# A small transformer layer with routed experts: the attention step's products, transposes and copies in another order

## The reference

```
h = gamma * norm(word[ids] + pos + type[types]) + beta       # eps 1e-12
a = norm(h)
q, k, v = a @ Wq, a @ Wk, a @ Wv         # 16 heads of 16
q, k = headnorm(q) * qw + qb, headnorm(k) * kw + kb
attn = softmax(causal(q k^T / 4))
h = h + (attn @ v) @ Wo + bo
x = norm(h)
scores = softmax(x @ gate^T); the 2 best experts of scores + bias
h = h + sum of the two: score * (silu(xs @ w1[e]) * (xs @ w3[e])) @ w2[e],  xs = x * score
```

## Time and profile before

| | |
|---|---|
| median of 3 runs | 560.64 us (559.51 to 562.48) |
| the profiled execution | 562.17 us |
| its span, first to last instruction | 560.0 us |
| mean granted TensorE clock | 0.958 |
| attention steps with scores | 29.9 to 201.8 us of the span |
| experts | from about 244 us on |

### The profile page before, as it was taken

How to read it: one execution, slowest core, us unless ns; L and a number is a source line. 1 busy time by engine, 2 the same in 40 slices (tenths; PEclk the granted TensorE clock), 3 DMA queues, 4 the chain that set the end, 5 groups by cost and what they waited for, 6 DMA issues and landing times.

```text
span 560.0 us, 12788 instructions
## 1 busy us (share of the span) xinstructions
PE 509.3 (91%) x4212; PEld 431.8 (77%) x4213; DVE 286.1 (51%) x710; ACT 258.1 (46%) x591; POOL 270.3 (48%) x503
## 2 busy tenths in 40 slices
PE   6788999999999886289999999999999999999991
PEld 2345767776777674169999999999999999999981
DVE  3686888788887656933333333333333333333330
ACT  1068899989988872043223332233322333322320
POOL 4587786777663201142444444443444444444432
PEclk9899999999999986589999999999999999999996
DMA  4017611000137673001211222112221122222221
GB/s 161 9 51 270 205 39 57 28 28 28 56 123 226 198 228 121 20 29 30 32 28 37 38 38 36 24 35 38 38 38 28 29 38 38 38 29 29 37 38 20
DMA packets 29480, 36.62 MB, mean 65 GB/s; under 512 B 7792, under 2 KB 23024, under 8 KB 29456
## 3 DMA queue, kind: packets, MB, share of 16 engines
q0 software_dynamic: 8352, 12.76, 13.3%
q1 hardware_dynamic: 20288, 22.51, 12.3%
q10 hardware_dynamic: 816, 1.06, 0.5%
HBM read 26.81 MB, written 9.50 MB: 65 GB/s over the span
## 4 chain that ended last, share of the span: by engine, by line
PE 81%; DVE 6%; POOL 3%; issue 3%; DMA 3%; ACT 3%; ACTq 0%; POOLq 0%; DVEq 0%
PE PS L1276 34%; PE PS L1287 18%; PE PS L1060 10%; PE PS L1146 7%; PE PS L1227 3%; PE PS L1107 3%; PE PS L1122 2%; PE PS L1099 2%; DMA x_pair<-word_dram,idx 1%; ACT work L566 1%; PE PS L1159 1%; DMA out_dram<-x_pair,dst_c 1%; DVE front L785 1%; DMA work<-x_rows,src_c 1%; POOL rstd L398 1%
## 5 line engine op out<-in xcount | busy, mean ns | idle before, releaser
L1276 PEld LDWEIGHTS PS<-work,arena 128*128 128x128 f32 x1716 | 197.6, 192 | 3.8 <-ACT work L670 2.0
L1276 PE MATMUL PS<-work,arena 128*128 128x128 f32 x1716 | 198.1, 276 | 1.5 <-ACT work L670 1.5
L676 ACT ACTIVATE work<-PS 128x768 f32<-128x768 f32 x39 | 31.6, 810 | 197.2 <-PE PS L1276 197.2
L1287 PE MATMUL PS<-w_sb,work 128*128 x468 | 107.6, 380 | 0.7 <-DVE x_pair L1035 0.7
L1027 DVE TENSOR_TENSOR work<-work,PS 128x640 f32<-128x640 f32 x39 | 32.0, 822 | 139.5 <-ACT work L676 139.5
L1287 PEld LDWEIGHTS PS<-w_sb,work 128*128 128x128 f32 x468 | 86.1, 191 | 11.0 <-issue 1.1
L513 POOL DMA_INDIRECT out_dram<-x_pair,dst_c x39 | 79.9, 2048 | 22.0 <-POOL dst_c L512 20.5
L566 ACT ACTIVATE work<-PS,nmax 128x128 f32<-128x128 f32 x256 | 72.5, 403 | 4.5 <-DVE nmax L795 4.5
L512 POOL COPY dst_c<-dest_i 128x1 int32 (+1 forms) x39 | 7.1, 182 | 137.2 <-DVE x_pair L1035 134.9
L666 ACT ACTIVATE arena<-w_sb 128x1408 f32 x40 | 55.1, 1377 | 17.8 <-DVE er_i L1000 12.8
L1060 PE MATMUL PS<-ident,work 128*128 128x128 f32 x336 | 56.5, 283 | 2.8 <-ACT work L566 2.6
(11 more groups left out here) (147 smaller groups left out, 610.4 us busy)
## 6 DMA issues: line engine op xcount, KB each, us to landing
w_sb<-w_dram SPq DMA_DIRECT2D x16, 640.0 KB, 6.2
w_sb<-w_dram SPq DMA_DIRECT2D x8, 704.0 KB, 4.7
x_rows<-x SPq DMA_DIRECT2D x16, 128.0 KB, 1.9
out_dram<-arena SPq DMA_DIRECT2D x16, 128.0 KB, 2.1
w_sb<-w_dram SPq DMA_DIRECT2D x16, 64.0 KB, 6.3
w_sb<-w_qkv_dram ACTq DMA_DIRECT2D x1, 768.0 KB, 7.9
work<-x_rows,src_c POOLq DMA_INDIRECT x41, 2.8
out_dram<-x_pair,dst_c POOLq DMA_INDIRECT x39, 4.2
```

The lines of the kernel that those rows point to most:

```text
L1276: last = n.matmul(up_ps[p][:, i, c, :], ws[p][:, k, at:at + P], xT_sb[p][:, k, :], start=(k == 0), stop=(k == DK - 1))
L1287: last = n.matmul(PS[:, 7, 0:D], hT_sb[p][:, i, :], w2_sb[:, bass.ds(e, 1), i, :], start=(i == 0), stop=(i == FK - 1))
```

## The change

- **Banks.** The transposes of `a_n` go to the right half of `VY_BANK`. `outputs` no longer waits for `aT_ready`, but for `var_f`, the reader of the output product in the right half of `O_BANK`, in every step; the rows' transposes and `values` wait for each other's readers in `VY_BANK` (`v_ready`, `aT_ready`).
- **TensorE's order.** The q and k product stands ahead of `outputs`; `outputs_back` goes behind `keys_to_rows(1)` and `x2_to_rows`; the output product goes ahead of the mask product of bank 1.
- **ScalarE's order.** After the exponentials of banks 0 and 1: `squares`, `queries_and_keys_out`, `outputs_out` (before: the other way round). `normalized_out` goes ahead of `transposed(1)`.
- **VectorE's order.** `squared_sums` goes ahead of the reciprocal and the product for `o_n`.
- **Last bank.** Each of the first three exponentials of bank 3 signals `exp_group`, the last one `exp_done` as before, and each of TensorE's four transposes waits for its own.

```diff
@@ -203,3 +203,3 @@
         qkn_ready, qk_ps, qk_ready = sem("qkn_ready"), sem("qk_ps"), sem("qk_ready")
-        s_done, max_done, exp_done = sem("s_done"), sem("max_done"), sem("exp_done")
+        s_done, max_done, exp_done, exp_group = sem("s_done"), sem("max_done"), sem("exp_done"), sem("exp_group")
         probsT_ps, probsT_ready, pv_done, o_ready = (
@@ -567,2 +567,4 @@
                                             bias=nmax[:, c:c + 1])
+                        if r == RG - 1 and g < GROUPS - 1:
+                            last.then_inc(exp_group, 1)
                     last.then_inc(exp_done, 1)
@@ -615,3 +617,3 @@
                     wait(act, v_done, u - 1)
-                    a.activation(aT[p].rearrange("p k s -> p (k s)"), PS[:, O_BANK, 0:D],
+                    a.activation(aT[p].rearrange("p k s -> p (k s)"), PS[:, VY_BANK, D:2 * D],
                                  ACT.Copy).then_inc(aT_ready, 1)
@@ -620,8 +622,8 @@
                     exponentials(1)
-                if valid(t - 1):
-                    outputs_out(t - 1)
-                if valid(t + 1):
-                    queries_and_keys_out(t + 1)
                 if valid(t + 2):
                     squares(t + 2)
+                if valid(t + 1):
+                    queries_and_keys_out(t + 1)
+                if valid(t - 1):
+                    outputs_out(t - 1)
                 if valid(t):
@@ -632,3 +634,2 @@
                     exponentials(2)
-                    transposed(1)
                 if valid(t - 1):
@@ -636,2 +637,3 @@
                 if valid(t):
+                    transposed(1)
                     exponentials(3)
@@ -903,2 +905,4 @@
                     centered(t + 4, p)
+                if valid(t + 2) and valid(t):
+                    squared_sums(t + 2)
                 u = t - 1
@@ -912,4 +916,2 @@
                                     spread(rden[:, :], 2, HD), ALU.mult).then_inc(o_ready, 1)
-                if valid(t + 2) and valid(t):
-                    squared_sums(t + 2)
                 if at_step(t, B + 1):
@@ -1115,5 +1117,3 @@
                     pe.wait_ge(v_ready, u + 1)
-                    wait(pe, aT_ready, u + 4)
-                    if edge and t + 2 >= B:
-                        wait(pe, var_f, u)
+                    wait(pe, var_f, u)
                     wait(pe, oT_ready, u)
@@ -1136,8 +1136,15 @@
 
-                    pe.wait_ge(exp_done, RG * t + r + 1)
-                    if r == RG - 1:
+                    if r < RG - 1:
+                        pe.wait_ge(exp_done, RG * t + r + 1)
+                        transposes(probs[:, r * 512:(r + 1) * 512], GROUPS, r).then_inc(probsT_ps, 1)
+                    else:
                         wait(pe, logits_read, t - 1)
                         wait(pe, qk_ready, t + 2)
-                    transposes(probs[:, r * 512:(r + 1) * 512], GROUPS,
-                               T_BANK if r == RG - 1 else r).then_inc(probsT_ps, 1)
+                        for g in range(GROUPS):
+                            if g < GROUPS - 1:
+                                pe.wait_ge(exp_group, (GROUPS - 1) * t + g + 1)
+                            else:
+                                pe.wait_ge(exp_done, RG * t + r + 1)
+                            last = transposes(probs[:, r * 512 + g * P:r * 512 + (g + 1) * P], 1, T_BANK, g * P)
+                        last.then_inc(probsT_ps, 1)
 
@@ -1164,3 +1171,6 @@
 
-                    pe.wait_ge(aT_ready, u + 1)
+                    if isinstance(u, int) and u == 0:
+                        pe.wait_ge(aT_ready, 1)
+                    else:
+                        wait(pe, aT_ready, u + 2)
                     wait(pe, v_ready, u)
@@ -1182,5 +1192,5 @@
                     pe.wait_ge(a_ready, u + 1)
-                    wait(pe, var_f, u - 3)
                     wait(pe, aT_ready, u)
-                    transposes(a_n, DK, O_BANK).then_inc(aT_ps, 1)
+                    wait(pe, v_ready, u - 1)
+                    transposes(a_n, DK, VY_BANK, D).then_inc(aT_ps, 1)
                 u = t + 1
@@ -1192,4 +1202,2 @@
                     transposes(qkn, 2 * DK, T_BANK).then_inc(qk_ps, 1)
-                if valid(t - 1):
-                    outputs(t - 1)
                 u = t + 2
@@ -1199,6 +1207,6 @@
                     project(u, aT[p], QK_BANK, 0, 2 * D, qk_done)
+                if valid(t - 1):
+                    outputs(t - 1)
                 if valid(t):
                     keys_to_rows(0)
-                if valid(t - 1):
-                    outputs_back(t - 1)
                 if valid(t):
@@ -1207,2 +1215,4 @@
                     x2_to_rows(t - 2)
+                if valid(t - 1):
+                    outputs_back(t - 1)
                 if valid(t + 1) and valid(t):
@@ -1219,4 +1229,2 @@
                     keys_to_rows(2)
-                if valid(t + 1) and valid(t):
-                    mask_bank(t + 1, 1)
                 u = t - 1
@@ -1229,2 +1237,4 @@
                     last.then_inc(wo_done, 1)
+                if valid(t + 1) and valid(t):
+                    mask_bank(t + 1, 1)
                 if at_step(t, B - 2):
```

More of the change, by code:

```diff
@@ L620, in step @@
                     exponentials(1)
+                if valid(t + 2):
+                    squares(t + 2)
+                if valid(t + 1):
+                    queries_and_keys_out(t + 1)
                 if valid(t - 1):
                     outputs_out(t - 1)
-                if valid(t + 1):
-                    queries_and_keys_out(t + 1)
-                if valid(t + 2):
-                    squares(t + 2)
                 if valid(t):
```

## The result

| | before | after |
|---|---|---|
| median, on the same chip | 561.22 us (4 runs) | 565.86 us (4 runs) |
| ratio | | 1.0094, 95% interval 1.0075 to 1.0113 |
| profiled execution, its span | 562.17, 560.0 us | 565.83, 563.6 us |
| scores of step 2, 14, 15 at | 56.06, 189.58, 200.68 us | 56.49, 194.04, 205.30 us |
| twelve steps (2 to 13) | 133.52, 11.13 each | 137.55, 11.46 each |

The account below looks back on a forecast made before the run. Bound: a ring through nearly full ScalarE and TensorE, 11.08 us a step. At +0.31, twelve steps give 3.7, step 1 0.3, steps 14 and 15 about 0: sum +4.0, forecast 564.5 us, range 559 to 568.5.

Parts of the forecast that it names:

- The ring: Attention step: scores, rows' transposes, aT copy, in all 8.43 us of ScalarE back to back, last transposes, masks; 11.08 us.
- Part 1: Rows' transposes into the value bank: the 0.25 us wait for the aT copy stays and changes owner, worth 0.
- Part 2: q and k product first, ending at 4.06 after the scores: ScalarE's squares stall 0.16 us for it.
- Part 3: ScalarE's new order: squares, q and k copies, then outputs' copy, which ends at 6.56 instead of 4.58.
- Part 4: Outputs' way back: transposes back start at 6.62, normalized outputs at 8.08 instead of 7.44; moved squared sums cost nothing.
- Part 5: Rest of TensorE's step after the normalized outputs start: 3.31 us instead of 3.64, since 0.33 of waits go.
- Part 6: Single signals for the last bank: worth 0.12 us a step, already counted; their own cost taken as 0.
- Rival D: Last bank: the single signals do nothing, up to 0.12 us a step more, 566 us; counted within the forecast's 0.53.
- Steps 1, 14, 15: Steps outside the twelve: step 1 0.3 us longer, steps 14 and 15 together 0 or a little less.
- Rival A: Attention step: no change, 11.08 us again or up to 0.2 more; 560 to 563 us, chance 0.28.
- B: Transposes back: outputs' copy ends by 6.3, TensorE's own work sets steps of 10.6 to 10.7; 556 us, chance 0.09.
- Rival C, its second half: Step 15: bank 1's transposes keep the granted clock up, 1.5 to 2 us saved; 563 us, chance 0.04.

Follow-up runs that it names:

- e7: e6 with the q and k product put ahead of the outputs' product on TensorE alone, ScalarE's order as before: 572.32 us, ratio to before 1.0216.
- e9: The change without the bank move, the normalized rows' transposes back in the outputs' bank: 565.98 us, ratio to before 1.0104.
- e1: The kernel before with only the normalized rows' transposes moved to the value bank: 561.33 us, ratio to before 1.0004.
- e5: The change with the outputs' transposes back put ahead of the x2 transposes on TensorE: 568.43 us, ratio to before 1.0148.
- e11: The change with the outputs' copy on VectorE, centering and x2 copy later, transposes back ahead of x2's: 563.34 us, ratio to before 1.0043.
- e10: The change with the sums of squares back behind the outputs' product on VectorE: 571.95 us, ratio to before 1.0207.
- e4: The change without the single signals, the last bank waited for as a whole: 569.32 us, ratio to before 1.0157.
- e2: The kernel before with only the single signals and waits of the last bank: 560.11 us, ratio to before 0.9987.
- e3: The kernel before with both the bank move and the single signals, old order: 559.17 us, ratio to before 0.9980.
- e6: The change with the old order of the two products and what hangs on it put back: 557.46 us, ratio to before 0.9943.
- e8: e6 with the x2 copy moved from ScalarE to VectorE, behind the outputs' product: 560.76 us, ratio to before 0.9992.

## Why the prediction was right, step by step

**The forecast held** (slower; +4.0 us forecast, +4.6 measured, in the range), and so did its chain in the steps: 11.39 forecast for one like step 8, 11.41 measured. The terms outside these steps held less well, see below.

- *What bounds the kernel.* The ring aT copy, ScalarE, last transposes: e7 confirms it, where a stall of 0.99 on ScalarE came back as 1.09 a step.
- *Part 1, the bank: 0.* e9 shows it for the new order (11.46 either way), e1 for the old (ratio 1.0004). The rule to rotate banks from the Trainium skill (Perfetto Trace Analysis, section Matmuls), which the forecast weighed at −3 us, gives nothing in either: new, because the next group reads what the copy writes; old, because the TensorE time won ahead was waited away behind.
- *Part 2, the stall ahead of the squares: 0.16.* Measured 0.11: the eight exponentials keep ScalarE for 2.01 (124.86 to 126.87 in the earlier trace rows), from 127.09 to 129.10, and the squares start at 129.21.
- *Part 3, the outputs' copy ends at 6.56: "the expensive part".* Measured 6.49; e5 and e11 show that this copy holds the way back, and nothing else of TensorE's.
- *Part 4, 6.62 and 8.08.* Measured 6.55 and 8.01. That the moved sums cost nothing is right, but it is half of it. They had to move: left in place they would have cost another 0.55 a step (e10). The forecast asked what their new place costs, never what the old one would.
- *Part 5, the rest 3.31.* Measured 3.40. The output product and bank 3 did give their waits back (0.87 and 0.44 from start to start, for 1.04 and 0.49). 0.06 of the 0.09 is at the normalized outputs' transposes, which follow a wait now and take 0.28 from start to start, for 0.22. That ScalarE's copy to `oT` would wait 0.3 to 0.5 for them was too much: it is 0.20.
- *Part 6, 0.12 a step for the signals, their own cost 0.* e4: 0.09 in the new order; e2: 0.06 in the old; 0.11 or 0.12 in both outside the hardware loop. Rival D falls.
- *Steps 1, 14, 15.* 0.43 up to step 2 for 0.3 is luck: step 1 did not get longer but 0.77 shorter, while the scores of step 0 came 2.15 later, which the forecast had not looked at. Steps 14 and 15 were forecast at 0 together; step 14 cost 0.16, near the 0.2 by which its outputs were to come later. **The term that failed is step 13**: 0.83 where 0.31 stood. The sum took all twelve steps as equal and left out that in one of them VectorE has 2.1 us of routing work (2.3 after the change) between the logits and the normalization of q and k, with nothing to spare.
- *Rival A* (11.08 again) falls, and *B* with it: it needed the outputs' copy by 6.3, and it was there at 6.49. e11 brought the transposes back to 5.87 by other means, and even so the step was 11.11 and not 10.6.
- *Rival C, its second half,* looks as if it had come true: after scores 15 the clock was 1.00 for over 10 us, and the tail 1.3 us shorter. But e2, which keeps TensorE's old order, had 1.00 in the same place, 207 to 209 with scores 15 at 198.12:

```profile
207.00:209.00 2.00, 1.06 (x12) 0.68 (x10) 2.00 (x3) 1.39 (x4) 0.00 (x0) 1.00 1.04 395
```

So the moved transposes of bank 1 are not needed for it. Nor is it e2 alone: in all twelve other profiles, five of them with `outputs` first as before (e1, e2, e3, e6, e8), the clock stays at 1.00 for at least 11 us after scores 15. Only in the profile of before does it fall 5 us after them. The 0.50 in the earlier trace rows is thus a trait of that execution, and what brings it on stays open. By the Trainium skill (TensorE: Matmul & The Clock Gate, Part 4: PE-mode transpose), transposes don't count as TensorE being busy for its clock; no run here tests that rule.

## What to carry to other kernels

When a step is a ring (each piece waits for the one before it, and the last for the first of the next step) through two engines that are both nearly full, price a reorder by what each result is waited for, and follow the piece that is moved back, not the one that is moved forward: here a product came 1.2 us earlier for which no engine had waited, and a copy came 1.9 us later on which the end of the step hung. List the other rings too, here the one over GpSimd: they have little to spare, and a move that looks free is either what keeps them short or what makes them the bound. And look at the steps that aren't like the others, for their engines have no slack to take a shift of half a microsecond.

## What the runs showed of the chip

- ScalarE's results come later where its queue has had no gap. In step 8 of e3, where it has none, the copies and squares of 128x512 take 0.65, 0.68, 0.69, 0.74 and 0.80 in their order, and the exponentials of banks 2 and 3 take 1.25 and 1.31 to their last result; in e11, which has gaps of 0.1 and 0.3 in its step, bank 3's exponentials took 1.15 and a copy of that size 0.59 to 0.63. From start to start a copy keeps ScalarE for 0.48 in both. So a handover from a full ScalarE costs 0.1 us or more (an estimate from these rows) that its throughput doesn't show. Why is open.
- A TENSOR_TENSOR of 128x64 on VectorE (its routing work) takes 0.47 to 0.49 us where GpSimd is in its own TENSOR_TENSOR of 128x256 (L431) at the same time, 0.22 or 0.23 where GpSimd is in its 128x32 operations. That holds for all eight of steps 11 and 12 that meet L431 (in the change, e4, e5 and e9) and for the eighteen of the other nine profiles that don't. The overlap is what the rows show; no run varies it alone. L746 above is one of them; GpSimd's L431 runs from 180.16 to 180.89 there.
- The steps of the kernel before that run in the hardware loop alternated between 11.08 and 11.21 us (for instance 122.94, 134.02, 145.23); those outside it took 11.08 to 11.11. In e1, with another bank and the same order, the loop's steps were 11.08 to 11.11. What the 0.13 is was not found out.
- The time of the profiled execution up to the scores of step 2 differs between executions of kernels that are the same up to there but for the bank: 56.49 in the change, 55.05 in e9. The granted clock was 0.50 from 18 to 20 us in the change (and in the kernel before), and 1.00 in e9. Under 1%, steps read from the trace tell more than the total of one execution.
